# Another order for a fused cross-attention and ternary feed-forward kernel: slots, reading engines and warm-up products rearranged

## The reference

```python
x = x + xattn(layernorm(x), ctx, Wq, Wkv_expand, Wout)
x = x + ffn(layernorm(x), w_gate, w_up, w_down)
```

## Time and profile before

| what | value |
|---|---|
| median of 3 runs | 96.84 us (96.61 to 97.01) |
| the profiled execution's own time | 97.0 us |
| its span (first to last instruction) | 95.3 us |
| busy: PE, DVE, ACT, POOL | 79.4, 68.4, 57.1, 51.4 us |
| start of the scores, slots 0 to 7 | 11.96, 18.21, 25.18, 29.90, 39.28, 44.05, 49.97, 54.37 us |
| first transposition of slot 8, first gate and up product | 60.15, 63.46 us |

### The profile page before, as it was taken

One profiled execution on the slowest core, in us unless ns is written; L12 is line 12 of the kernel. 1 busy time (PEld: TensorE's weight loads), 2 busy tenths in 40 slices (PEclk: granted clock), 3 DMA queues, 4 the chain that ended last, 5 costly groups with the idle time before them and its releaser, 6 DMA issues.

```text
span 95.3 us, 2459 instructions
## 1 busy us (share of the span) xinstructions
PE 79.4 (83%) x895; PEld 56.7 (60%) x895; DVE 68.4 (72%) x169; ACT 57.1 (60%) x103; POOL 51.4 (54%) x107
## 2 busy tenths in 40 slices
PE   4997796985999559999999997799945879998580
PEld 1365572855687548787977775766322547656370
DVE  4642847789592850798958999375999999999641
ACT  0622339493259973677587962586729387996610
POOL 5620271145945972397947962525186272587550
PEclk9999999999999999999999999999999999999999
DMA  1799999200000000000811826000000000011123
GB/s 18 195 327 363 349 353 393 86 0 0 0 0 7 3 0 7 0 7 7 187 33 30 197 68 152 0 7 0 0 0 0 0 0 0 9 57 55 55 98 122
DMA packets 11747, 7.59 MB, mean 80 GB/s; under 512 B 6552, under 2 KB 11480, under 8 KB 11736
## 3 DMA queue, kind: packets, MB, share of 16 engines
q1 hardware_dynamic: 11068, 6.93, 24.3%
q10 hardware_dynamic: 668, 0.51, 1.9%
HBM read 4.95 MB, written 0.92 MB: 62 GB/s over the span
## 4 chain that ended last, share of the span: by engine, by line
PE 45%; DVE 24%; ACT 12%; issue 8%; DMA 6%; ACTq 2%; POOL 1%; DVEq 0%
PE bank L889 26%; DVE amax L808 9%; PE sc L889 8%; DVE h_sb L801 7%; DMA wq_sb<-in_L_xattn_Wq_dram 6%; PE bank L1020 6%; ACT v_wide L560 4%; PE bank L1044 3%; ACT pT L375 2%; ACT k_wide L339 2%; ACT tern L587 2%; DVE s_tok L815 1%; ACT xnT L560 1%; DVE shifted L715 1%; ACTq L311 1%
## 5 line engine op out<-in xcount | busy, mean ns | idle before, releaser
L889 PE MATMUL sc<-wT,xqT 128*128 128x512 bf16 x56 | 13.9, 380 | 3.4 <-DVE h_sb L801 3.4
L300 POOL TENSOR_SCALAR wf_sb<-h_sb,r_tok 128x512 f32<-128x512 f32 x13 | 9.2, 718 | 10.4 <-DVE r_tok L822 10.4
L450 POOL TENSOR_SCALAR veps<-mv 128x1 f32<-128x1 f32 x13 | 2.5, 192 | 20.2 <-DVE mv L669 14.1
L607 ACT ACTIVATE wf_sb<-sc,s_out 128x512 f32<-128x512 f32 x14 | 9.6, 689 | 5.9 <-PE sc L889 3.6
L706 DVE TENSOR_REDUCE mx<-sc 128x16 f32<-128x896 f32 x8 | 8.7, 1090 | 3.8 <-PE sc L889 3.7
L801 DVE SCALAR_TENSOR_TENSOR h_sb<-sc,s_out,wf_sb 128x512 f32<-128x512 f32 x14 | 9.9, 740 | 1.1 <-ACT wf_sb L607 1.1
L889 PE MATMUL bank<-xnT,wqT 128*128 128x224 f32 (+1 forms) x40 | 7.4, 329 | 3.6 <-ACT xnT L560 2.2
L889 PEld LDWEIGHTS sc<-wT,xqT 128*128 128x128 bf16 x56 | 5.0, 98 | 9.2 <-DVE h_sb L801 5.1
L889 PEld LDWEIGHTS bank<-v_wide,pT 128*64 128x64 f32 x256 | 8.1, 138 | 2.3 <-issue 2.3
L889 PEld LDWEIGHTS bank<-xnT,wqT 128*128 128x128 f32 x40 | 6.2, 190 | 5.0 <-issue 3.4
L889 PE MATMUL bank<-v_wide,pT 128*64 128x34 f32 x256 | 9.0, 225 | 0.0
(11 more groups left out here) (107 smaller groups left out, 167.4 us busy)
## 6 DMA issues: line engine op xcount, KB each, us to landing
wf_sb<-in_L_ffn_w_gate_dram SPq DMA_DIRECT2D x1, 1024.0 KB, 9.2
wf_sb<-in_L_ffn_w_up_dram SPq DMA_DIRECT2D x1, 1024.0 KB, 11.5
wf_sb<-in_L_ffn_w_down_dram SPq DMA_DIRECT2D x1, 1024.0 KB, 11.9
out_dram<-k_wide SPq DMA_DIRECT2D x7, 128.0 KB, 1.7
x_sb<-in_x_dram SPq DMA_DIRECT2D x1, 512.0 KB, 6.7
x_sb<-in_x_dram SPq DMA_DIRECT2D x1, 256.0 KB, 5.6
wq_sb<-in_L_xattn_Wq_dram ACTq DMA_DIRECT2D x1, 256.0 KB, 5.7
wo_sb<-in_L_xattn_Wout_dram SPq DMA_DIRECT2D x1, 256.0 KB, 9.4
```

Of the source, the lines that this page charges most:

```text
L300: ops.tensor_scalar(h_int[:, t % 2, c, :], h_sb[:, t % 3, GC * c:GC * c + GC], r_tok[:, 1, t:t + 1], CODED, ALU.mult, ALU.add).then_inc(hi ...
L607: nc.scalar.activation(g_sb[:, t % 2, GC * c:GC * c + GC], SC[:, j % 4, :], ACT.Silu, scale=s_out[:, 0, t:t + 1]).then_inc(silu_ready, 1)
L889: return nc.tensor.matmul(*a, **k)
```

## The change

Only tables at the head of the file change; every function stays as it is. The instructions are the same in kind and nearly in number; what changes is their slot, their order in a slot, and for some the engine: the sum of the gate weights goes from DVE to ACT, the reads of eight products go from ACT to DVE and those of three from DVE to ACT, and the last half of the last tile's rounding goes from POOL to DVE.

```diff
-AMAX_SLOTS = [4, 5, 6, 7, 8, 10, 11]
-XQ_SLOTS = [5, 6, 7, 8, 10, 12, 13]
-LN1_SLOTS = {-1: [1, 2], 0: [3], 1: [4], 2: [5], 3: [6]}
-ABS_SLOTS = {(1, 'vector'): [0], (2, 'scalar'): [1], (3, 'scalar'): [2]}
-MEAN_SLOTS = [2, 3, 4]
-ROUND_SLOTS = [3, 3, 4, 4, 5, 5]
-SIGN_SLOTS = [4, 4, 5, 5, 6, 6]
+AMAX_SLOTS = [4, 5, 6, 7, 8, 9, 10]
+XQ_SLOTS = [5, 6, 9, 9, 9, 11, 12]
+LN1_SLOTS = {-1: [1, 2, 3, 4], 0: [], 1: [5], 2: [], 3: [6]}
+ABS_SLOTS = {(1, 'scalar'): [0], (2, 'scalar'): [1], (4, 'scalar'): [2]}
+MEAN_SLOTS = [3, 4, 5]
+ROUND_SLOTS = [3, 4, 4, 5, 5, 6]
+SIGN_SLOTS = [6, 6, 6, 7, 7, 7]
-WARM_MORE = {('wkvT', 1): 3, ('ctxT', 0): 1}
+WARM_MORE = {('ctxT', 0): 0, ('ctxT', 1): 0, ('k', 0, (0, 1), (0, 1)): 1, ('q', 0, 1): 1,
+ ('wkvT', 0): 0, ('wkvT', 1): 2, ('wqT', 0): 0, ('xT', 0): 0}
-MISC_JOBS = {-1: [('wkvT', 0), ('wkvT', 1), ('ctxT', 0), ('wqT', 0), ('k', 0, K_FIRST, (0, 1)), ('xT', 0), ('q', 0, 1), ('ctxT', 1)],
-             0: [('xT', 1), ('k', 0, K_REST, (0,)), ('k', 1, K_ALL, (0,)), ('k', 0, K_REST, (1,)), ('k', 1, K_ALL, (1,)),
-                 ('q', 1, 2), ('v', 0), ('v', 2)],
-             1: [('xT', 2), ('xT', 3), ('q', 2, 4)],
-             2: [('v', 1), ('v', 3)],
-             3: [('woT', 0), ('xT', 4), ('xT', 5), ('q', 4, 6)],
+MISC_JOBS = {-1: [('wkvT', 0), ('wkvT', 1), ('ctxT', 0), ('k', 0, (0, 1), (0, 1)), ('xT', 0), ('wqT', 0), ('ctxT', 1), ('q', 0, 1),
+      ('k', 0, (1, 4), (0,))],
+ 0: [('xT', 1), ('k', 1, (0, 4), (1,)), ('k', 1, (0, 4), (0,)), ('k', 0, (1, 4), (1,)), ('q', 1, 2), ('v', 0), ('v', 2),
+     ('xT', 2), ('xT', 3)],
+ 1: [('q', 2, 4)],
+ 2: [('v', 1), ('v', 3), ('xT', 5)],
+ 3: [('xT', 4), ('woT', 0), ('q', 4, 6)],
-VECTOR_READS = [('wkvT', 1), ('ctxT', 0), ('k', 0, K_FIRST, (0, 1)), ('k', 0, K_REST, (1,)), ('k', 1, K_ALL, (1,))]
-SUB_BEHIND = {0: 2, 1: 2}
+VECTOR_READS = [('k', 0, (0, 1), (0, 1)), ('k', 0, (1, 4), (1,)), ('xT', 2), ('v', 3), ('xT', 0), ('v', 0), ('xT', 1), ('xT', 4),
+ ('woT', 0), ('wkvT', 0)]
+SUB_BEHIND = {0: 1, 1: 2, 2: 0, 3: 7}
-WIDENINGS = {2: [(1, 0, 0), (1, 1, 0)],
-             3: [(1, 0, 1), (1, 1, 1)]}
+WIDENINGS = {0: [(1, 1, 1)], 1: [(1, 0, 1)], 2: [(1, 0, 0), (1, 1, 0)], 3: []}
 ROUNDER = [...
-           ('gpsimd', 'gpsimd'), ('vector', 'gpsimd')]
+ ('gpsimd', 'gpsimd'), ('vector', 'vector')]
```

More of the change, by code:

```diff
@@ L22 @@
 OP_SLOTS = [3, 4, 5, 6, 7, 8, 9]
-AMAX_SLOTS = [4, 5, 6, 7, 8, 10, 11]
-XQ_SLOTS = [5, 6, 7, 8, 10, 12, 13]
-LN1_SLOTS = {-1: [1, 2], 0: [3], 1: [4], 2: [5], 3: [6]}
-ABS_SLOTS = {(1, 'vector'): [0], (2, 'scalar'): [1], (3, 'scalar'): [2]}
-MEAN_SLOTS = [2, 3, 4]
-ROUND_SLOTS = [3, 3, 4, 4, 5, 5]
-SIGN_SLOTS = [4, 4, 5, 5, 6, 6]
-WARM_PRODUCTS = 9
-WARM_MORE = {('wkvT', 1): 3, ('ctxT', 0): 1}
+AMAX_SLOTS = [4, 5, 6, 7, 8, 9, 10]
[5 more added lines that the diff above has]
+SIGN_SLOTS = [6, 6, 6, 7, 7, 7]
+WARM_PRODUCTS = 9
+WARM_MORE = {('ctxT', 0): 0,
+ ('ctxT', 1): 0,
+ ('k', 0, (0, 1), (0, 1)): 1,
+ ('q', 0, 1): 1,
+ ('wkvT', 0): 0,
+ ('wkvT', 1): 2,
+ ('wqT', 0): 0,
+ ('xT', 0): 0}
 X_PARTS = [(0, 1), (1, 3), (3, 7)]
@@ L37 @@
 K_FIRST, K_REST, K_ALL = (0, 1), (1, 4), (0, 4)
-MISC_JOBS = {-1: [('wkvT', 0), ('wkvT', 1), ('ctxT', 0), ('wqT', 0), ('k', 0, K_FIRST, (0, 1)), ('xT', 0), ('q', 0, 1), ('ctxT', 1)],
-             0: [('xT', 1), ('k', 0, K_REST, (0,)), ('k', 1, K_ALL, (0,)), ('k', 0, K_REST, (1,)), ('k', 1, K_ALL, (1,)),
-                 ('q', 1, 2), ('v', 0), ('v', 2)],
-             1: [('xT', 2), ('xT', 3), ('q', 2, 4)],
-             2: [('v', 1), ('v', 3)],
-             3: [('woT', 0), ('xT', 4), ('xT', 5), ('q', 4, 6)],
-             4: [('xT', 6)],
-             5: [('q', 6, 8)]}
-VECTOR_READS = [('wkvT', 1), ('ctxT', 0), ('k', 0, K_FIRST, (0, 1)), ('k', 0, K_REST, (1,)), ('k', 1, K_ALL, (1,))]
-SUB_BEHIND = {0: 2, 1: 2}
+MISC_JOBS = {-1: [('wkvT', 0), ('wkvT', 1), ('ctxT', 0), ('k', 0, (0, 1), (0, 1)), ('xT', 0), ('wqT', 0), ('ctxT', 1), ('q', 0, 1),
[5 more added lines that the diff above has]
+ 3: [('xT', 4), ('woT', 0), ('q', 4, 6)],
+ 4: [('xT', 6)],
+ 5: [('q', 6, 8)]}
+VECTOR_READS = [('k', 0, (0, 1), (0, 1)), ('k', 0, (1, 4), (1,)), ('xT', 2), ('v', 3), ('xT', 0), ('v', 0), ('xT', 1), ('xT', 4),
+ ('woT', 0), ('wkvT', 0)]
+SUB_BEHIND = {0: 1, 1: 2, 2: 0, 3: 7}
 WIDE = [('k', 0, K_FIRST, (0, 1)), ('k', 0, K_REST, (0,)), ('k', 0, K_REST, (1,))]
 KEY_GROUPS = [[], [(0, 2), (2, 4)]]
-WIDENINGS = {2: [(1, 0, 0), (1, 1, 0)],
-             3: [(1, 0, 1), (1, 1, 1)]}
+WIDENINGS = {0: [(1, 1, 1)], 1: [(1, 0, 1)], 2: [(1, 0, 0), (1, 1, 0)], 3: []}
 ROUNDER = [('gpsimd', 'gpsimd'), ('gpsimd', 'gpsimd'), ('gpsimd', 'gpsimd'), ('gpsimd', 'gpsimd'), ('gpsimd', 'gpsimd'),
-           ('gpsimd', 'gpsimd'), ('vector', 'gpsimd')]
+ ('gpsimd', 'gpsimd'), ('vector', 'vector')]
 FINISHER = ['gpsimd', 'gpsimd', 'gpsimd', 'gpsimd', 'gpsimd', 'vector', 'vector']
```

## The result

The changed kernel takes **92.83 us** (median of 4 runs, 92.17 to 93.19), the kernel before, measured beside it, 96.93 us (96.61 to 97.08). The ratio is 0.957, with a 95% interval of 0.953 to 0.961. Forecast were 92.7 us and a range of 91.8 to 95.2. The profiled execution of the changed kernel took 93.19 us, with a span of 91.5 us; the 1.7 us around the span are the same as before.

A forecast was written before the change was run, and what follows sets the result against it. PE was taken to bound the kernel, idle 5.90 us between first scores and first gate product. 0.40 + 0.45 + 1.43 + 1.96 - 0.23 + 0.10 = 4.1 us off 97.0, less 0.16 to the median, gave 92.7 us; range 91.8 to 95.2.

The forecast's parts named there:

- VectorE becomes the bound: Rival, slots 0 to 3: a v read on DVE costs 1.4 instead of 0.68 us, giving 94.7 us; chance 0.14.
- Slots 0, 1 and 3: PE's idle time there mostly goes: 0.45 us won in slot 0, 1.43 in slot 1, 1.96 in slot 3.
- Slot -1: Work before the first scores, reordered: taken as 0, bounds -0.3 and +0.3 us, wqT's later read offsetting xT's earlier one.
- PE's work before q is the same: Slot -1: the reordering leaves PE's work ahead of q unchanged; q waits for the later read of wqT and xT.
- K's second product fills the time in which PE waited: Slot -1: moved behind q, it covers ACT's read of q; its absence from slot 0 gains an estimated 0.40 us.
- The signs: Slots 6 and 7, three each: aT reads come late, PE loses 0.45 us, net -0.23 after two code transpositions leave.
- ScalarE's signs come back: Rival: weight transpositions issued closer together share, the second landing up to 2.7 us after the gate product is ready; 94.0 us, chance 0.14.
- The codes of tiles 5 and 6: Slots 8 on: POOL's rounding waits for PE, tile 5's y_sb comes some 2.2 us later; cost 0, margin 0.5 us.
- +0.10 at the end: Last tile: DVE rounds both halves, 0.49 us each, so the second half is ready about 0.1 us sooner.
- The waits change their names only: Rival, slots 1 and 3: other reads take the 1.43 and 2.26 us of idle time; 96.7 us, chance 0.06.
- The lower level of TensorE: Rival: PE falls back to 1.2 GHz through slot 0, its 5.35 us of work doubling at most; 98.1 us, chance 0.06.

## Why the prediction was right, point by point, and where it was not

**The mechanism was right.** The idle time of PE in slots 0, 1 and 3 was a matter of order, and the change took it away. "VectorE becomes the bound" fell by its price: a v read on DVE took 0.75 us where I had taken 0.68 and feared 1.4. The Trainium skill ("Perfetto Trace Analysis", Optimizing Scalar/DVE Operations) puts the overhead of a PSUM read on DVE at some 125 ns against 51 on ACT, by which a read would be 74 ns longer on DVE, an estimate. The trace agrees in sign and shows a little over half of that: 746 against 703 ns for a v read.

**Slots 0, 1 and 3 were sized too small.** Slots 0 and 1 gave 2.72 us, where 0.40, 0.45 and 1.43 had been forecast, 2.28; of slot 0's idle time nothing stayed. I had looked for what would be late next in slot 0 and not for what its 0.90 us were: a wait for ACT's read of K's second product, which went with the product (in the run with the start of before 0.72 us of it are back). For the move of that product I had counted its 0.40 us alone. Slot 3 gave 2.39 instead of 1.96; the 0.30 us that I left for woT behind ACT's read of aT did not occur (0.08 idle). Part of what was left over is PE's own work, which fell by 0.72 us and not by 0.40 + 0.22 = 0.62 (K's second product and two transpositions of codes).

**Slot -1, taken at 0 with bounds of 0.3, is the step that failed.** The new order cost 0.75 us for the same end of the Wkv transpositions; over the profiles with this head the scores began at 12.73 us in the mean (12.30 to 13.27, seven of them), over three of before at 11.89. In the pair compared first that cost is hidden by the wait for Wq's load: the DMA's 6% of the chain are the wait for that load, which the prediction put aside. I had put the later read of wqT against the earlier one of xT and missed two things: K, now first, waits 0.56 us for the read of ctxT with PE idle, and the second context transposition moved ahead of q, so that "PE's work before q is the same" was wrong. "K's second product fills the time in which PE waited" was right only in part, since the old order had filled it already. Against that stands 1.1 us in slot 0, so the move of the start as a whole is a gain of some 0.3 us in the profile, too small for the times, which do not tell the two starts apart (92.66 and 92.83 us).

**The signs** (forecast -0.45, less 0.22 for the transpositions of codes that leave) cost nothing, and the codes gave 0.15 to 0.17. I had counted ACT's lateness without looking whether DVE, which sets those slots, is later still. The rival "ScalarE's signs come back" fell with them. The DMA transpositions of the gate and up weights in the changed kernel, and below them that of the down weights, against the earlier trace rows:

```profile
DMA to landing us min/median/max: 3.7/3.8/4.0
...
DMA to landing us min/median/max: 5.3/5.3/5.3
```

The two that the gate product needs, issued 3.2 us apart, landed after 3.70 and 3.95 us, hardly later than before; the second was there at 58.80 us, 12.5 us after slot 6 began (forecast 12.7), and the gate product at 59.60 us followed pv(7) without a wait. Something of the sharing that the rival feared shows only in the third, issued 2.1 us after the second: it took 5.3 instead of 3.6 us, and nothing waited for it, since the first down projection comes ten microseconds after it landed.

**The codes of tiles 5 and 6** did what was forecast: POOL's rounding waited 4.61 us for PE, and its y_sb was done at 64.43, before DVE came to it at 64.67. The margin was 0.24 us, not 0.5. The profile even credits these tables with 0.26 us behind the gate product (32.16 less 31.90), and the tail ate it: **+0.10 at the end became -0.33** (31.57 less 31.90). I had added two DVE roundings of 0.49 us; the second took 0.97 (85.57 to 86.54), beside POOL's addition at 85.53. In the run with POOL's half, POOL's 0.98 us, against a mean of 0.69 for such a half in the changed kernel, ran beside DVE's 0.49. The Trainium skill ("SBUF — State Buffer", Who interferes with whom) says that DVE and GpSimd share a pair of ports, and that with some DVE instructions, tensor_scalar among them, the one that issues first has the pair for its whole length and the other waits. The direction agrees with these rows, where each time the later starter was the longer one; that the port is the cause was not tried.

**What the sum left out** is that its terms are not independent. The weights' tables alone: 0. All but these tables: 2.1% of the 4.3%. All but the split of reads: 2.1%. Each part uncovers a wait that another part removes: with PE earlier in slot 1, DVE's sum of 2.25 us is next, which I had costed only on ACT's side, and with xT(5) in slot 2 the scale product there puts pv(1) behind a v read. "The waits change their names only" was judged by idle time of DVE and ACT as a whole; for a single part it is what happened. The gain came because all parts came together; that the total met the forecast is the sum of larger gains (5.11 instead of 4.1) and of a start that cost what had been put at 0, and nothing in the prediction made them meet: luck. `LN1_SLOTS`, `WIDENINGS` and `SUB_BEHIND` were not undone by themselves, and the split of the reads was not tried alone; what they are worth so is open.

**Slips in the working**, none of which turns the forecast. In slot 0, 17.26 less 16.91 leaves 0.35 and not 0.45 us. The low end of the range, 92.7 less 0.98, is 91.7. The two DVE rows behind the price of a v read are 1.16 and 1.37 ns an element and do not agree on 1.2. "The waits change their names only" takes away 1.96 and 1.43 us, which gives 96.1 and not 96.7.

**The lower level of TensorE** did not come in slot 0: PE was busy for 5.83 of 5.83 us there and q's eight products took 1.15 us, as in slot 0 of the profile of before.

The times that were to show it, 18.1, 22.9, 27.6 and 35.0 us for scores 1 to 4 and 59.4 for the gate product, came as 19.10, 23.77, 28.54, 35.53 and 59.60. Each carries the 1.31 us of the late start, which the larger gains use up step by step.

## What to carry to other kernels

Where several engines are each late by a little, cost a reordering as a whole: after each wait that goes, ask for every other engine when it comes to the same place, since a part alone may be worth nothing and half the gain be lost without it. An idle stretch at the start is filled by something already; moving work into it is paid in the order of what it displaces. Before a second instruction on one engine is counted at the duration of the first, look at what runs beside it on the other.

## What the runs showed of the hardware

The kernel's first products are the same in every run, and yet the 16 Wkv transpositions, which begin between 4.79 and 5.22 us with 9 products on zeroed data ahead of them, took 1.09 to 1.69 us in the kernel before and 1.09 to 1.97 with the head of the changed one, although the granted clock reads 1.00 in these stretches. The products on zeroed data have 512 columns each. In the second repetition of the kernel before, those ahead of the transpositions started 0.43 us apart (2.10, 2.52, 2.95 us), the rate of 1.2 GHz, and those behind them 0.22 us apart (7.07, 7.29 us), that of 2.4 GHz. In the first profile of before the last two of the nine were already only 0.26 us apart, and in the run with seven products the two behind the transpositions still 0.40 (6.27, 6.67 us). So the rise from 1.2 to 2.4 GHz comes at another moment in each execution, sometimes ahead of these transpositions and sometimes within or behind them. The first scores follow it (on top came, in the first profile of before, a wait of 0.48 us for the load of Wq, and in the run with the signs spread out some 0.2 us for that of the context), and with the changed head they spread from 12.30 to 13.27 us, as much as the times do, some 1 us. What decides the moment stays open.

The DMA transposition of a weight matrix took 3.6 to 3.9 us from issue to landing when the one before it had been issued 4.5 us or more earlier (the first profile of before, the run with the signs spread out), and 5.3 us when it had been issued 2.1 us earlier (the changed kernel, twice, and the run with the codes undone).
